# Macaron block on one core: Gram products of the projection stage in bursts of eight chunks instead of four, and the turns at a tile's end in another order

## The chip, the cores and the metric

The kernel is one program on one core of a Trainium2 chip. The metric is device time in microseconds (us) of one execution, and lower is better. Five engines run their own instruction streams and meet at semaphores: TensorE (PE in the profile, PEld for its weight loads), VectorE (DVE), ScalarE (ACT), GpSimd (POOL) and SyncE (SP), which here only issues DMAs.

## What is computed

The input is `x` of 1 x 8192 x 512 in fp32. A block of three parts works on it:

```
x = x + 0.5 * ffn(layernorm(x))
x = x + attn_block(layernorm(x))
x = x + 0.5 * ffn(layernorm(x))

ffn(x):   s = x @ Win + bin                       # 512 -> 64
          h = relu(s[..., None] * W1 + b1)        # 16 per hidden unit
          g = sum(h * W2) + b2;  g @ Wout + bout  # 64 -> 512
attn_block(x): gated delta rule with 16 heads of 32:
          q, k, v = rmsnorm(x) @ wq, wk, wv;  k = k / |k|;  beta = sigmoid(... @ wbeta)
          per token:  S += beta * (v - S k) k^T;   o = S q
          x + o @ wo, and then a 512 -> 2048 -> 512 MLP with its own rmsnorm and residual
```

The delta rule is computed in chunks of 32 tokens. For each chunk and head the kernel needs two 32 x 32 products beforehand: `K (beta K)^T`, masked to one strict triangle with the sign turned, and `Q (beta K)^T`, masked to the other triangle with its diagonal. These are the Gram products of this case.

## The kernel before

The kernel has three stages, one after the other: projections (stage 1, to about 1190 us), the delta rule over chunks (stage 2), and the MLP with the second ffn (stage 3). The change touches stage 1 alone.

Stage 1 runs over 16 tiles of 512 tokens (`NT` = 16, `t` below). Every engine's order is written out by hand, and work of neighbouring tiles is interleaved. While TensorE projects tile `t`, it also does the first ffn of tile `t + 1` (`hidden`, `ffn_out`) and most Gram products of tile `t - 1`. The engines' parts for one tile are:

- TensorE: thirteen projections `project(t, 0)` to `project(t, 12)` of 12 matmuls each (beta, then v, q, k for each of the four head groups `g4`), in PSUM banks 0 to 2 in turn. `hidden(t + 1)` stands between projections 1 and 2. `ffn_out(t + 1)`, four blocks in banks 6, 7, 6, 7, follows project(t, 6). Gram bursts `gram(t - 1, n)` use banks 6 and 7 in turn: four before and after project(t, 4) (two each), the same around projections 7 and 10.
- At a tile's end a list, `TURNS`, sets the order of the transposes of the next tile's normalised rows (`turn_h`, "h"), of those of the tile after next (`turn_x`, "x"), and of the first four Gram bursts of tile `t` ("g"). All three engines walk through this list: TensorE does the transposes and Gram bursts, ScalarE `h_turned` and `x_turned`, VectorE `h_low` (for "h") and `mask` (for "g").
- VectorE: `mask(t, n)` multiplies the finished burst by the two triangles, two instructions of 128 columns (`ltb`, line 765, and `pb`, line 767). The bank is free for the next use once the second is done (`released[bk] = v_P, ...`). VectorE also does the ffn's sums over hidden units (`sums`, line 670), the transposes of v and k (`turn_v`, line 727, `turn_k`, line 734, `turn_kb`, line 756), bias and residual adds (`add_bout`, line 658, `add_ffn`, line 677) and key norms (`norms`, line 738).
- `h_low(t + 1, f)` (line 713) writes the low part of the next tile's projection operand and frees the bank of turn_h (banks 3, 4, 3, 5 for f = 0 to 3). Turns "x" use banks 5, 4, 3, 4. The next tile's projections need all four parts.
- SyncE: `store_gram(t)` writes `ltb` and `pb` out, 1 MB each, once the last mask of tile `t` is done; `store_v`, `store_q` of the next tile and `load_x` stand behind it in the same queue. `mask(t, 0)` overwrites the buffers and so waits for both stores of tile `t - 1`.

On TensorE a burst and its bank look so before the change:

```
bk, g4 = 6 + n % 2, n // 4
...
bank_free(bk)
for i in range(4):
    for h in range(4):
```

Of the kernel before, what the change touches and what calls it, by code (L numbers as in the profile page):

```python
# [12 lines left out]
P = 128  # L13
# [9 lines left out]
CH = 32  # L23
# [15 lines left out]
def shape_constants():  # L39
# [17 lines left out]

H_BANK, X_BANK, WIN_BANK = (3, 4, 3, 5), (5, 4, 3, 4), 5

TURNS = (("h", 0), ("h", 1), ("x", 0), ("g", 0), ("h", 2), ("g", 1), ("x", 1), ("h", 3),  # L60
         ("g", 2), ("x", 2), ("g", 3), ("x", 3))


def solver_slots(systems):
# [23 lines left out]
def macaron(nc, a, consts, out, x1_d, z_d, heads_d, lt_d, xt_d):  # L88
# [28 lines left out]
    with ExitStack() as top:  # L117
# [115 lines left out]
        def sp_project(e):  # L233

            def load_x(t):
                i = t % 2
                if t >= 2:
                    e.wait_ge(d_x1[i], 16 * (t // 2))
                    e.wait_ge(a_y1, 4 * (t - 1))
                e.dma_start(X[i][:, :, :], x_v[t]).then_inc(d_x[i], 16)  # L240

            def store_x1(t):
                e.wait_ge(v_x1, 4 * t + 4)
                e.dma_start(x1_v[t], X[t % 2][:, :, :]).then_inc(d_x1[t % 2], 16)
# [12 lines left out]
            def store_q(t):  # L257
                e.wait_ge(a_ev, 13 * t + PROJ_AT["q", 3] + 1)
                e.dma_start(slot(t, Q2), chunked(qk[:, 0, :, :, :])).then_inc(d_q, 16)

            def store_k(t):
                e.wait_ge(v_kn, 4 * t + 4)
                e.dma_start(slot(t, K2), chunked(kb2[t % 2][:, :, :, :])).then_inc(d_k, 16)

            def store_b(t):
                e.wait_ge(o_kb, 4 * t + 4)
                e.dma_start(slot(t, B2), chunked(kbuf[:, :, :, :])).then_inc(d_b, 16)

            def store_gram(t):
                e.wait_ge(v_lt, 16 * t + 16)  # L270
                e.dma_start(lt_d[t // 2, :, (t % 2) * TC:(t % 2 + 1) * TC, :, :], ltb[:, :, :, :]).then_inc(d_lts, 16)
                e.wait_ge(v_P, 16 * t + 16)
                e.dma_start(slot(t, P2), chunked(pb[:, :, :, :])).then_inc(d_p, 16)

            def load_weights(i):
                j = i % 8
                if i >= 8:
                    e.wait_ge(v_wlo, i - 8 + 1)
                e.dma_start(stage1[j], pieces1[i][0]).then_inc(d_stage[j], 16)

            def load_system0(t):
                n = group_in(t)
                if n is not None:
                    e.wait_ge(d_lts, 32)
                    e.wait_ge(p_win, min(t + 2, NT))
                    e.dma_start(lt0, lt_d[0, :, :, n, :]).then_inc(d_lt0, 16)

            def store_system0(t):
                n = group_out(t)
                if n is not None:  # L290
                    e.wait_ge(v_back0, n + 1)
                    e.dma_start(xt_d[:, :, n, :].rearrange("c p i -> p c i"), xt0).then_inc(d_xt0, 16)

            load_x(0)
            load_x(1)
            e.wait_ge(o_z, 2)
            e.dma_start(wbraw[:, :, :], a["L0_attn_wbeta"].rearrange("(k p) h -> p k h", p=P)).then_inc(d_w1, 16)
            for h in range(4):
                e.dma_start(bbeta[32 * h:32 * h + GROUPS, :],
                            a["L0_attn_bbeta"].rearrange("(g h o) -> h g o", h=4, o=1)[h], **SHORT).then_inc(d_w1, 16)  # L300
            for n in KINDS:
                e.dma_start(bias[n][:, :], a[f"L0_attn_b{n}"].rearrange("(g p) -> p g", p=P),
                            **SHORT).then_inc(d_w1, 16)
            e.dma_start(ln1[:, :], a["L0_attn_ln1_scale"].rearrange("(g p) -> p g", p=P), **SHORT).then_inc(d_w1, 16)
            for i in range(8):
                load_weights(i)
            store_x1(0)
            for i in range(8, 12):
                load_weights(i)
            for t in range(NT):  # L310
                if t + 2 < NT:
                    load_x(t + 2)
                load_system0(t)
                if t:
                    store_k(t - 1)
                    store_b(t - 1)
                if t + 1 < NT:
                    store_x1(t + 1)
                store_system0(t)
                if t:  # L320
                    store_gram(t - 1)
                store_v(t)
                store_q(t)
            store_k(NT - 1)
            store_b(NT - 1)
            store_gram(NT - 1)

        def pe_project(e):
# [58 lines left out]

            def gram(t, n):

                bk, g4 = 6 + n % 2, n // 4  # L390
                e.wait_ge(v_kbT, 4 * t + g4 + 1)
                e.wait_ge(v_KT, 4 * t + g4 + 1)
                e.wait_ge(a_ev, 13 * t + PROJ_AT["q", g4] + 1)
                bank_free(bk)
                for i in range(4):
                    for h in range(4):
                        r, c = slice(32 * h, 32 * h + 32), 4 * (n % 4) + i
                        m = e.matmul(bank[bk][r, i * WIDE:(i + 1) * WIDE].rearrange("p (s i) -> p s i", s=2),  # L398
                                     rawk[r, c, g4, :], qk[r, :, c, g4, :], start=True, stop=True)
                m.then_inc(p_gram, 1)  # L400
                released[bk] = v_P, 16 * t + n + 1

            e.wait_ge(d_par, PAR)
            e.wait_ge(a_half, 2)
# [8 lines left out]
            for t in range(NT):  # L413
# [5 lines left out]
                project(t, 3)  # L419
                for g4 in range(1, GROUPS):  # L420
                    if t:
                        gram(t - 1, 4 * g4)
                        gram(t - 1, 4 * g4 + 1)
                    project(t, 3 * g4 + 1)
                    if t:
                        gram(t - 1, 4 * g4 + 2)
                        gram(t - 1, 4 * g4 + 3)
                    project(t, 3 * g4 + 2)
                    project(t, 3 * g4 + 3)
                    if g4 == 1 and t + 1 < NT:  # L430
# [1 line left out]
                for what, n in TURNS:  # L432
# [3 lines left out]
                        turn_h(t + 1, n)  # L436
                    elif what == "x" and t + 2 < NT:
                        turn_x(t + 2, n)
            for n in range(4, 16):
                gram(NT - 1, n)  # L440

        def act_project(e):
# [49 lines left out]
            def evict(t, j):  # L492
# [14 lines left out]
                elif kind == "q":  # L507
                    if t:
                        e.wait_ge(d_q, 16 * t)
                        e.wait_ge(p_gram, 16 * (t - 1) + 4 * g4 + 4)  # L510
                    e.activation(qk[:, 0, :, g4, :], blocks(bank[bk][:, :]), ACT.Identity,
                                 bias=bias[kind][:, g4:g4 + 1]).then_inc(a_ev, 1)
                else:
                    if t:
                        e.wait_ge(p_gram, 16 * (t - 1) + 4 * g4 + 4)
                    elif g4 == 0:
                        e.wait_ge(v_wb, 1)
                    e.activation(rawk[:, :, g4, :], blocks(bank[bk][:, :]), ACT.Identity,
# [115 lines left out]
        def dve_project(e):  # L634
# [105 lines left out]
            def scale_k(t, g4):  # L740
# [7 lines left out]
                e.tensor_tensor(K, K, nrm[:, u].unsqueeze(2).broadcast_to([P, TC, HD]), ALU.mult).then_inc(v_kn, 1)  # L748
                e.wait_ge(v_kn, n + 1)
                if t:  # L750
                    e.wait_ge(p_gram, 16 * (t - 1) + 4 * g4 + 4)
                e.transpose(qk[:, 1, :, g4, :], K).then_inc(v_KT, 1)

            def turn_kb(t, g4):
# [1 line left out]
                e.transpose(rawk[:, :, g4, :], kbuf[:, :, g4, :]).then_inc(v_kbT, 1)  # L756

            def mask(t, n):
                g4, c = n // 4, slice(4 * (n % 4), 4 * (n % 4) + 4)
                gb = bank[6 + n % 2][:, 0:4 * WIDE].rearrange("p (u s i) -> p u s i", s=2, i=CH)  # L760
                e.wait_ge(p_gram, 16 * t + n + 1)
                if t:
                    e.wait_ge(d_lts, 16 * t)
                    e.wait_ge(d_p, 16 * t)
                e.tensor_tensor(ltb[:, c, g4, :], gb[:, :, 1, :], gmask[:, 0:1, :].broadcast_to([P, 4, CH]),
                                ALU.mult).then_inc(v_lt, 1)
                e.tensor_tensor(pb[:, c, g4, :], gb[:, :, 0, :], gmask[:, 1:2, :].broadcast_to([P, 4, CH]),  # L767
                                ALU.mult).then_inc(v_P, 1)

            def system0(t):  # L770
# [68 lines left out]
            for t in range(NT):  # L839
# [26 lines left out]
                system0(t)  # L866
                turn_k(t, 0)
                if t:
                    mask(t - 1, 4)
                    mask(t - 1, 5)  # L870
                turn_v(t, 1)
                if t + 2 < NT:
                    add_bout(t + 2, 1)
                if t + 1 < NT:
                    sums(t + 1, 6, 7)
                if t:
                    mask(t - 1, 6)
                    mask(t - 1, 7)
                    turn_kb(t - 1, 3)
                if t + 2 < NT:  # L880
                    add_bout(t + 2, 2)
# [4 lines left out]
                    add_ffn(t + 1)  # L886
                turn_k(t, 1)
                if t:
                    mask(t - 1, 8)
                    mask(t - 1, 9)  # L890
                turn_v(t, 2)
                scale_k(t, 0)
                if t + 1 < NT:
                    stats_x1(t + 1, 0)
                    stats_x1(t + 1, 1)
                if t:
                    mask(t - 1, 10)
                    mask(t - 1, 11)
                if t + 1 < NT:
                    stats_x1(t + 1, 2)  # L900
                    stats_x1(t + 1, 3)
# [4 lines left out]
                    shift1(t + 1)  # L906
                turn_k(t, 2)
                if t:
                    mask(t - 1, 12)
                    mask(t - 1, 13)  # L910
                turn_v(t, 3)
                if t + 1 < NT:
                    scale_h(t + 1, 0)
                    scale_h(t + 1, 1)
                scale_k(t, 1)
                if t:
                    mask(t - 1, 14)
                    mask(t - 1, 15)
                if t + 1 < NT:
                    scale_h(t + 1, 2)  # L920
                    scale_h(t + 1, 3)
# [9 lines left out]
            norms(NT - 1, 3)  # L931
            turn_kb(NT - 1, 2)
            scale_k(NT - 1, 3)
            for n in range(4, 12):
                mask(NT - 1, n)
            turn_kb(NT - 1, 3)
            for n in range(12, 16):
                mask(NT - 1, n)

        def pool_project(e):  # L940
# [1061 lines left out]
```

## Time and profile before

| | |
|---|---|
| runs | 3695.51 us median of 3 (3686.24 to 3698.28) |
| the profiled execution | 3692.6 us, span 3690.6 us |
| TensorE busy | 3364.3 us, 91% of the span |
| VectorE, ScalarE, GpSimd busy | 1886.2, 1327.8, 1147.5 us |
| mean granted TensorE clock | 0.962 of full speed |
| stage 1 | its TensorE work ends near 1182 us, stage 2 begins its products at 1194 us |

The profile is of one execution. Busy times overlap between engines and are no parts of a sum. An engine's row in a timeline gives its start, its duration, and in brackets how long the engine was idle before it and who ended that. One fp32 matmul appears as two records; 64 records of line 398 are two Gram bursts of before.

### The profile page before, as it was taken

How to read it: one execution, taken by the hardware profiler on the slowest of the kernel's cores; microseconds unless marked ns; L12 is line 12 of the kernel's file. 1: busy time of each engine (PE TensorE's matmuls, PEld its weight loads, DVE VectorE, ACT ScalarE, POOL GpSimd, SP SyncE). 2: the span in 40 equal slices, each digit the busy share in tenths (PEclk: the TensorE clock that was granted, in tenths of full speed). 3: DMA queues.
4: the chain of work that ended last, by engine and by line, in shares of the span. 5: the costliest groups of instructions: out<-in, count | busy, mean ns of one | idle time of the engine just before them, and what ended most of it. 6: DMA issues, size and time to landing. Idle time of an engine off the chain costs nothing. (4 is left out here: it accounts for less than half of the span.)

```text
span 3690.6 us, 150931 instructions
## 1 busy us (share of the span) xinstructions
PE 3364.3 (91%) x68430; PEld 2637.4 (71%) x68430; DVE 1886.2 (51%) x3292; ACT 1327.8 (36%) x2630; POOL 1147.5 (31%) x1207
## 2 busy tenths in 40 slices
PE   3988888888896899999997899999999999999997
PEld 2666666666665688888886677777777777777775
DVE  4767766667664887877832233332333333333323
ACT  4434333344331233333333333333333333333332
POOL 0334435354452655555520112221121122122211
PEclk7999999999998899999998999999999999999998
DMA  3244353444334666665655110001000111000000
GB/s 90 81 150 121 105 159 115 115 137 133 110 122 143 196 193 192 200 192 182 187 173 167 65 35 24 23 35 35 24 35 35 35 35 35 35 30 17 35 35 23
DMA packets 388102, 355.46 MB, mean 96 GB/s; under 512 B 58128, under 2 KB 320912, under 8 KB 384912
## 3 DMA queue, kind: packets, MB, share of 16 engines
q1 hardware_dynamic: 385632, 351.27, 30.4%
q8 instruction: 155, 2.54, 0.3%
q10 hardware_dynamic: 2224, 0.90, 0.1%
q14 instruction: 91, 0.75, 0.1%
HBM read 184.19 MB, written 153.09 MB: 91 GB/s over the span
## 5 line engine op out<-in xcount | busy, mean ns | idle before, releaser
L1784 DVE TENSOR_TENSOR glo<-gl,gh 128x512 fp32r<-128x512 f32 x256 | 195.1, 762 | 927.3 <-ACT gh L1691 927.2
L1687 ACT ACTIVATE gl<-bank,b1m 128x512 f32<-128x512 f32 x256 | 175.9, 687 | 796.4 <-PE bank L231 796.4
L229 PE MATMUL bank<-w_hi,gh 128*128 128x512 f32 x1024 | 410.6, 401 | 24.3 <-DVE glo L1784 24.3
L229 PE MATMUL bank<-h_hi,w_hi 128*128 128x512 f32 x1024 | 425.9, 416 | 4.0 <-DVE w_lo L1828 4.0
L231 PE MATMUL bank<-w_hi,glo 128*128 128x512 f32 x1024 | 406.7, 397 | 0.0
L230 PE MATMUL bank<-h_lo,w_hi 128*128 128x512 f32 x1024 | 406.4, 397 | 0.0
L231 PE MATMUL bank<-h_hi,w_lo 128*128 128x512 f32 x1024 | 406.3, 397 | 0.0
L230 PE MATMUL bank<-w_lo,gh 128*128 128x512 f32 x1024 | 405.5, 396 | 0.0
L398 PE MATMUL bank<-qk,rawk 32*32 32x64 f32 x8192 | 166.4, 230 | 117.9 <-DVE pb L767 110.6
L398 PEld LDWEIGHTS bank<-qk,rawk 32*32 32x32 f32 x8192 | 138.4, 114 | 172.2 <-issue 170.6
L970 POOL TENSOR_TENSOR nrm<-nrm,cst 128x16 f32<-128x16 f32 x64 | 185.6, 2900 | 198.1 <-DVE nrm L738 197.8
L229 PEld LDWEIGHTS bank<-w_hi,gh 128*128 128x128 f32 x1024 | 192.8, 188 | 75.4 <-DVE glo L1784 31.3
L1189 PE MATMUL bank<-ringA 32*32 32x32 f32 x16512 | 237.8, 196 | 7.0 <-issue 4.1
L229 PEld LDWEIGHTS bank<-h_hi,w_hi 128*128 128x128 f32 x1024 | 193.3, 189 | 59.0 <-issue 10.8
L230 PEld LDWEIGHTS bank<-h_lo,w_hi 128*128 128x128 f32 x1024 | 193.4, 189 | 55.0 <-issue 10.8
L231 PEld LDWEIGHTS bank<-w_hi,glo 128*128 128x128 f32 x1024 | 193.3, 189 | 47.0
L231 PEld LDWEIGHTS bank<-h_hi,w_lo 128*128 128x128 f32 x1024 | 193.2, 189 | 46.2
L230 PEld LDWEIGHTS bank<-w_lo,gh 128*128 128x128 f32 x1024 | 193.6, 189 | 44.8
L1189 PEld LDWEIGHTS bank<-ringA 32*32 32x32 f32 x16512 | 198.4, 105 | 10.9 <-issue 4.4
L1878 POOL TENSOR_TENSOR ss<-ss,cst 128x4 f32<-128x4 f32 x16 | 16.3, 1017 | 576.4 <-DVE ss L1767 576.4
L1466 POOL TENSOR_TENSOR zb<-zb,bo 128x512 f32<-128x512 f32 x64 | 91.0, 1422 | 334.0 <-ACT zb L1332 334.0
L1391 DVE TENSOR_TENSOR tmp<-sysf 128x90 f32<-128x90 f32 (+14 forms) x210 | 184.5, 879 | 5.0
(172 smaller groups left out, 7214.8 us busy)
## 6 DMA issues: line engine op xcount, KB each, us to landing
ringB<-heads_scratch SPq DMA_DIRECT2D x256, 192.0 KB, 2.7
ringA<-heads_scratch SPq DMA_DIRECT2D x258, 128.0 KB, 2.2
X<-in_L_attn_x SPq DMA_DIRECT2D x16, 1024.0 KB, 9.7
x_scratch<-X SPq DMA_DIRECT2D x16, 1024.0 KB, 5.5
heads_scratch<-vb SPq DMA_DIRECT2D x16, 1024.0 KB, 11.3
heads_scratch<-qk SPq DMA_DIRECT2D x16, 1024.0 KB, 11.0
heads_scratch<-kb SPq DMA_DIRECT2D x16, 1024.0 KB, 5.2
heads_scratch<-kbuf SPq DMA_DIRECT2D x16, 1024.0 KB, 7.7
```

The lines of the kernel that those rows point to most:

```text
L229: e.matmul(o, lhs[0], rhs[0], start=first, stop=False)
L230: e.matmul(o, lhs[0], rhs[1], start=False, stop=False)
L231: return e.matmul(o, lhs[1], rhs[0], start=False, stop=last)
L398: m = e.matmul(bank[bk][r, i * WIDE:(i + 1) * WIDE].rearrange("p (s i) -> p s i", s=2), rawk[r, c, g4, :], qk[r, :, c, g4, :], start=True, ...
L970: e.tensor_tensor(nrm[:, u], nrm[:, u], pos_half.broadcast_to([P, TC]), ALU.pow).then_inc(o_pow, 1)
L1189: m = e.matmul(out[r, n, :], lhsT[r, n, :], rhs[r, n, :], start=first and n == 0, stop=True, skip_group_check=True)
L1391: e.tensor_tensor(tt, N[:, :, j + 1:CH, j:j + 1].broadcast_to([P, 3, rows, j]), N[:, :, j:j + 1, 0:j].broadcast_to([P, 3, rows, j]), ALU.m ...
L1466: e.tensor_tensor(zb[i][:, :], zb[i][:, :], bo[:, :], ALU.add).then_inc(o_yb, 1)
L1687: e.activation(gl[k][:, :], bank[k][:, :], ACT.Gelu_apprx_tanh, bias=b1m[:, m:m + 1]).then_inc(a_gl, 1)
L1784: e.tensor_tensor(gh[k][1][:, :], gl[k][:, :], gh[k][0][:, :], ALU.subtract).then_inc(v_gl, 1)
L1878: e.tensor_tensor(ss3[:, :], ss3[:, :], neg_half, ALU.pow).then_inc(o_ms, 1)
```

## The change

A burst now takes eight chunks and fills its bank (512 columns), so a tile has `NG` = 8 bursts instead of 16, two for each head group. Even `n` goes to bank 6 and odd `n` to bank 7, so the two halves of a group stand in different banks. The mask instructions are 256 columns wide, and there are half as many. Only the first chunk of a burst carries the start flag. In `TURNS` there are two bursts instead of four, and the second stands behind all four "h". The stores and the waits on `p_gram` count in eights.

```diff
-TURNS = (("h", 0), ("h", 1), ("x", 0), ("g", 0), ("h", 2), ("g", 1), ("x", 1), ("h", 3),
-         ("g", 2), ("x", 2), ("g", 3), ("x", 3))
+TURNS = (("h", 0), ("h", 1), ("x", 0), ("g", 0), ("h", 2), ("x", 1), ("h", 3), ("g", 1), ("x", 2), ("x", 3))
+
+NG = 2 * GROUPS
...
-                bk, g4 = 6 + n % 2, n // 4
+                bk, g4 = 6 + n % 2, n // 2
...
-                for i in range(4):
+                for i in range(8):
                     for h in range(4):
-                        r, c = slice(32 * h, 32 * h + 32), 4 * (n % 4) + i
+                        r, c = slice(32 * h, 32 * h + 32), 8 * (n % 2) + i
...
-                                     rawk[r, c, g4, :], qk[r, :, c, g4, :], start=True, stop=True)
+                                     rawk[r, c, g4, :], qk[r, :, c, g4, :], start=i == 0, stop=True,
+                                     skip_group_check=True)
                 m.then_inc(p_gram, 1)
-                released[bk] = v_P, 16 * t + n + 1
+                released[bk] = v_P, NG * t + n + 1
...
                     if t:
-                        gram(t - 1, 4 * g4)
-                        gram(t - 1, 4 * g4 + 1)
+                        gram(t - 1, 2 * g4)
                     project(t, 3 * g4 + 1)
                     if t:
-                        gram(t - 1, 4 * g4 + 2)
-                        gram(t - 1, 4 * g4 + 3)
+                        gram(t - 1, 2 * g4 + 1)
...
-                e.tensor_tensor(ltb[:, c, g4, :], gb[:, :, 1, :], gmask[:, 0:1, :].broadcast_to([P, 4, CH]),
+                e.tensor_tensor(ltb[:, c, g4, :], gb[:, :, 1, :], gmask[:, 0:1, :].broadcast_to([P, 8, CH]),
...
-            for n in range(4, 12):
+            for n in range(2, 6):
                 mask(NT - 1, n)
             turn_kb(NT - 1, 3)
-            for n in range(12, 16):
+            for n in range(6, NG):
                 mask(NT - 1, n)
```

TensorE in the middle of tile 1, around project(1, 4) (the matmuls on `wv_hi`; rows of its other matmuls left out), before. Each burst is 16 matmuls, the waits stand in brackets, and `v_P` is the mask that frees the bank:

```order
L398 MATMUL bank6<-qk,rawk 32x64 [waits a_ev,v_P,v_KT,v_kbT]
L398 MATMUL bank6<-qk,rawk 32x64 x15
L398 MATMUL bank7<-qk,rawk 32x64 [waits a_ev,v_P,v_KT,v_kbT]
L398 MATMUL bank7<-qk,rawk 32x64 x15
L229 MATMUL bank2<-hT_hi,wv_hi 128x512 [waits a_ev,v_lo]
...
L398 MATMUL bank6<-qk,rawk 32x64 [waits a_ev,v_P,v_KT,v_kbT]
L398 MATMUL bank6<-qk,rawk 32x64 x15
L398 MATMUL bank7<-qk,rawk 32x64 [waits a_ev,v_P,v_KT,v_kbT]
L398 MATMUL bank7<-qk,rawk 32x64 x15
L229 MATMUL bank0<-hT_hi,wq_hi 128x512 [waits a_ev,v_lo]
```

The same place of the change:

```order
L399 MATMUL bank6<-qk,rawk 32x64 [waits a_ev,v_P,v_KT,v_kbT]
L399 MATMUL bank6<-qk,rawk 32x64 x31
L230 MATMUL bank2<-hT_hi,wv_hi 128x512 [waits a_ev,v_lo]
...
L399 MATMUL bank7<-qk,rawk 32x64 [waits a_ev,v_P,v_KT,v_kbT]
L399 MATMUL bank7<-qk,rawk 32x64 x31
L230 MATMUL bank0<-hT_hi,wq_hi 128x512 [waits a_ev,v_lo]
```

The matmuls ahead of and behind project(1, 4) are as many as before, but the burst behind it goes to bank 7, which was last used at the end of the tile before and not by the burst ahead of it.

TensorE at the end of tile 0, from the first Gram burst of the list on to the next tile's first matmul, before (`cst,Y1` is a turn "h", `cst,Y0` a turn "x"):

```order
L398 MATMUL bank7<-qk,rawk 32x64 x15
L341 MATMUL bank4<-cst,Y0 128x128 [waits v_lo,a_y0]
L341 MATMUL bank4<-cst,Y0 128x128 x3
L350 MATMUL bank5<-cst,Y1 128x128 [waits a_xT,v_h]
L350 MATMUL bank5<-cst,Y1 128x128 x3
L398 MATMUL bank6<-qk,rawk 32x64 [waits a_ev,v_P,v_KT,v_kbT]
L398 MATMUL bank6<-qk,rawk 32x64 x15
L341 MATMUL bank3<-cst,Y0 128x128 [waits v_lo,a_y0]
L341 MATMUL bank3<-cst,Y0 128x128 x3
L398 MATMUL bank7<-qk,rawk 32x64 [waits a_ev,v_P,v_KT,v_kbT]
...
L229 MATMUL bank1<-hT_hi,wb_hi 128x512 [waits a_ev,v_lo]
```

And in the change:

```order
L342 MATMUL bank4<-cst,Y0 128x128 [waits v_lo,a_y0]
L342 MATMUL bank4<-cst,Y0 128x128 x3
L351 MATMUL bank5<-cst,Y1 128x128 [waits a_xT,v_h]
L351 MATMUL bank5<-cst,Y1 128x128 x3
L399 MATMUL bank7<-qk,rawk 32x64 [waits a_ev,v_x1,v_KT,v_kbT]
L399 MATMUL bank7<-qk,rawk 32x64 x31
L342 MATMUL bank3<-cst,Y0 128x128 [waits v_lo,a_y0]
L342 MATMUL bank3<-cst,Y0 128x128 x3
L342 MATMUL bank4<-cst,Y0 128x128 [waits a_xT,a_y0]
L342 MATMUL bank4<-cst,Y0 128x128 x3
L230 MATMUL bank1<-hT_hi,wb_hi 128x512 [waits a_ev,v_lo]
```

The last burst moved ahead of the last two "x", and no burst of the list waits any more for a mask of the same list; the third "x" still waits for the third `h_low` (`v_lo`).

VectorE at the same tile's end, from the first two `h_low` on, before:

```order
L713 SCALAR_TENSOR_TENSOR hT_lo<-bank,ln,hT_hi 128x512 [waits a_hi] x2
L765 TENSOR_TENSOR ltb<-bank,cst 128x4x32 [waits p_gram]
L767 TENSOR_TENSOR pb<-bank,cst 128x4x32
L713 SCALAR_TENSOR_TENSOR hT_lo<-bank,ln,hT_hi 128x512 [waits a_hi]
L765 TENSOR_TENSOR ltb<-bank,cst 128x4x32 [waits p_gram]
L767 TENSOR_TENSOR pb<-bank,cst 128x4x32
L713 SCALAR_TENSOR_TENSOR hT_lo<-bank,ln,hT_hi 128x512 [waits a_hi]
```

And in the change:

```order
L713 SCALAR_TENSOR_TENSOR hT_lo<-bank,ln,hT_hi 128x512 [waits a_hi] x2
L765 TENSOR_TENSOR ltb<-bank,cst 128x8x32 [waits p_gram]
L767 TENSOR_TENSOR pb<-bank,cst 128x8x32
L713 SCALAR_TENSOR_TENSOR hT_lo<-bank,ln,hT_hi 128x512 [waits a_hi] x2
L765 TENSOR_TENSOR ltb<-bank,cst 128x8x32 [waits p_gram]
L767 TENSOR_TENSOR pb<-bank,cst 128x8x32
```

One mask, now twice as wide, still stands between the second and the third `h_low`, as before; the one between the third and the fourth is gone.

## Rows read from the trace of the kernel before

**Rows 1.** The page, busy time: us, share, instructions

```profile
PE 3364.3 (91%) x68430; PEld 2637.4 (71%) x68430; DVE 1886.2 (51%) x3292; ACT 1327.8 (36%) x2630; POOL 1147.5 (31%) x1207
```

**Rows 2.** Waits of stage 1, 80 to 1180 us: total, times, longest

```profile
PE bank L398 <- DVE pb L767: 110.6, 32, 6.8
...
DVE ltb L765 <- DMA heads_scratch<-pb: 55.6, 15, 4.7
...
PE bank L367 <- DVE X L677: 15.2, 14, 1.1
...
PE bank L398 <- DVE X L677: 2.9, 14, 0.2
```

**Rows 3.** Timeline of TensorE, middle of tile 7: start, duration, idle before

```profile
561.62 0.40 PE L231 MATMUL bank<-hT_hi,wv_lo 128*128 128x512 f32 x1
566.05 1.93 PE L398 MATMUL bank<-qk,rawk 32*32 32x64 f32 x64 [4.04 <-DVE pb L767]
...
575.02 1.88 PE L367 MATMUL bank<-wout,g 128*128 128x512 f32 x4
577.99 1.98 PE L367 MATMUL bank<-wout,g 128*128 128x512 f32 x4 [1.09 <-DVE X L677]
```

**Rows 4.** Timeline of VectorE, the same stretch of tile 7

```profile
565.46 0.25 DVE L765 TENSOR_TENSOR ltb<-bank,cst 128x128 f32<-128x128 f32 x1
...
566.23 0.68 DVE L727 STREAM_TRANSPOSE vb<-proj 128x512 f32<-128x512 f32 x1
566.84 0.64 DVE L658 TENSOR_TENSOR X<-X,boutb 128x512 f32<-128x512 f32 x1
567.41 1.59 DVE L670 SCALAR_TENSOR_TENSOR g<-relu,w2t,g 128x512 f32<-128x512 f32 x2
568.92 0.28 DVE L765 TENSOR_TENSOR ltb<-bank,cst 128x128 f32<-128x128 f32 x1
...
569.72 0.70 DVE L756 STREAM_TRANSPOSE rawk<-kbuf 128x512 f32<-128x512 f32 x1
573.85 0.69 DVE L658 TENSOR_TENSOR X<-X,boutb 128x512 f32<-128x512 f32 x1 [3.43 <-ACT Y L449]
```

**Rows 5.** Windows from the waiting burst to ffn_out's third block, tiles 1 to 13: length, busy, clock

```profile
221.07:230.78 9.71, 8.62 (x92) 1.00 0.30 88
...
711.44:724.01 12.57, 11.48 (x92) 0.75 0.00 1
...
sum 150.69, PE 136.54; mean PE 10.50
```

**Rows 6.** Timeline of TensorE, middle of tile 14, the last with an ffn_out

```profile
1061.38 1.10 PE L398 MATMUL bank<-qk,rawk 32*32 32x64 f32 x64 [1.76 <-DVE pb L767]
```

**Rows 7.** Timeline of TensorE, end of tile 7

```profile
610.42 0.65 PE L398 MATMUL bank<-qk,rawk 32*32 32x64 f32 x32 [3.45 <-DVE pb L767]
...
613.13 0.78 PE L229 MATMUL bank<-hT_hi,wb_hi 128*128 128x512 f32 x1
```

**Rows 8.** Timeline of SyncE's queue, end of tile 7: the store of P

```profile
600.86 0.44 SPq L273 DMA_DIRECT2D heads_scratch<-pb  x1
```

**Rows 9.** Timeline of VectorE, end of tile 7

```profile
609.78 0.29 DVE L765 TENSOR_TENSOR ltb<-bank,cst 128x128 f32<-128x128 f32 x1 [4.53 <-DMA heads_scratch<-pb]
...
610.19 0.74 DVE L713 SCALAR_TENSOR_TENSOR hT_lo<-bank,ln,hT_hi 128x512 fp32r<-128x512 f32 x1
```

**Rows 10.** Windows of 7 us behind a tile-end wait (two) and behind ffn_out's wait (one): clock is the fourth number

```profile
540.86:547.86 7.00, 6.99 (x93) 1.00 0.98 280
...
1035.73:1042.73 7.00, 7.00 (x81) 0.55 0.81 238
...
577.99:584.99 7.00, 6.77 (x120) 1.00 0.40 152
```

**Rows 11.** Timeline of VectorE, end of stage 1

```profile
1157.62 0.29 DVE L765 TENSOR_TENSOR ltb<-bank,cst 128x128 f32<-128x128 f32 x1 [4.20 <-DMA heads_scratch<-pb]
...
1168.00 0.25 DVE L765 TENSOR_TENSOR ltb<-bank,cst 128x128 f32<-128x128 f32 x1
...
1182.02 0.28 DVE L767 TENSOR_TENSOR pb<-bank,cst 128x128 f32<-128x128 f32 x1
```

More of the change, by code:

```diff
@@ L269, in store_gram @@
             def store_gram(t):
-                e.wait_ge(v_lt, 16 * t + 16)
+                e.wait_ge(v_lt, NG * t + NG)
                 e.dma_start(lt_d[t // 2, :, (t % 2) * TC:(t % 2 + 1) * TC, :, :], ltb[:, :, :, :]).then_inc(d_lts, 16)
-                e.wait_ge(v_P, 16 * t + 16)
+                e.wait_ge(v_P, NG * t + NG)
                 e.dma_start(slot(t, P2), chunked(pb[:, :, :, :])).then_inc(d_p, 16)
@@ L438, in pe_project @@
                         turn_x(t + 2, n)
-            for n in range(4, 16):
+            for n in range(2, NG):
                 gram(NT - 1, n)
@@ L509, in evict @@
                         e.wait_ge(d_q, 16 * t)
-                        e.wait_ge(p_gram, 16 * (t - 1) + 4 * g4 + 4)
+                        e.wait_ge(p_gram, NG * (t - 1) + 2 * g4 + 2)
                     e.activation(qk[:, 0, :, g4, :], blocks(bank[bk][:, :]), ACT.Identity,
@@ L514, in evict @@
                     if t:
-                        e.wait_ge(p_gram, 16 * (t - 1) + 4 * g4 + 4)
+                        e.wait_ge(p_gram, NG * (t - 1) + 2 * g4 + 2)
                     elif g4 == 0:
@@ L750, in scale_k @@
                 if t:
-                    e.wait_ge(p_gram, 16 * (t - 1) + 4 * g4 + 4)
+                    e.wait_ge(p_gram, NG * (t - 1) + 2 * g4 + 2)
                 e.transpose(qk[:, 1, :, g4, :], K).then_inc(v_KT, 1)
@@ L758, in mask @@
             def mask(t, n):
-                g4, c = n // 4, slice(4 * (n % 4), 4 * (n % 4) + 4)
-                gb = bank[6 + n % 2][:, 0:4 * WIDE].rearrange("p (u s i) -> p u s i", s=2, i=CH)
-                e.wait_ge(p_gram, 16 * t + n + 1)
+                g4, c = n // 2, slice(8 * (n % 2), 8 * (n % 2) + 8)
+                gb = bank[6 + n % 2][:, :].rearrange("p (u s i) -> p u s i", s=2, i=CH)
+                e.wait_ge(p_gram, NG * t + n + 1)
                 if t:
@@ L764, in mask @@
                     e.wait_ge(d_p, 16 * t)
-                e.tensor_tensor(ltb[:, c, g4, :], gb[:, :, 1, :], gmask[:, 0:1, :].broadcast_to([P, 4, CH]),
+                e.tensor_tensor(ltb[:, c, g4, :], gb[:, :, 1, :], gmask[:, 0:1, :].broadcast_to([P, 8, CH]),
                                 ALU.mult).then_inc(v_lt, 1)
-                e.tensor_tensor(pb[:, c, g4, :], gb[:, :, 0, :], gmask[:, 1:2, :].broadcast_to([P, 4, CH]),
+                e.tensor_tensor(pb[:, c, g4, :], gb[:, :, 0, :], gmask[:, 1:2, :].broadcast_to([P, 8, CH]),
                                 ALU.mult).then_inc(v_P, 1)
@@ L868, in dve_project @@
                 if t:
-                    mask(t - 1, 4)
-                    mask(t - 1, 5)
+                    mask(t - 1, 2)
                 turn_v(t, 1)
@@ L876, in dve_project @@
                 if t:
-                    mask(t - 1, 6)
-                    mask(t - 1, 7)
+                    mask(t - 1, 3)
                     turn_kb(t - 1, 3)
@@ L888, in dve_project @@
                 if t:
-                    mask(t - 1, 8)
-                    mask(t - 1, 9)
+                    mask(t - 1, 4)
                 turn_v(t, 2)
@@ L896, in dve_project @@
                 if t:
-                    mask(t - 1, 10)
-                    mask(t - 1, 11)
+                    mask(t - 1, 5)
                 if t + 1 < NT:
@@ L908, in dve_project @@
                 if t:
-                    mask(t - 1, 12)
-                    mask(t - 1, 13)
+                    mask(t - 1, 6)
                 turn_v(t, 3)
@@ L916, in dve_project @@
                 if t:
-                    mask(t - 1, 14)
-                    mask(t - 1, 15)
+                    mask(t - 1, 7)
                 if t + 1 < NT:
```

## The prediction

> **What bounds the kernel now.** I read the page first: TensorE is busy for 91% of the span [rows 1], so only its idle time, its slow stretches and the path that feeds it are worth anything. Stages 2 and 3 are untouched by the change. For stage 1 the next view is the list of waits. There, one wait stands out for TensorE: 110.6 us in 32 times until a mask's second instruction frees a Gram bank [rows 2]. The timeline shows that this comes twice a tile, at different places and for different reasons.
>
> The first place is the middle of the tile, in tiles 1 to 14. The bursts behind project(t, 4) need the banks of the bursts ahead of it. VectorE comes to those masks only behind its sums for the ffn. In tile 7 TensorE's last matmul before starts at 561.62 us and the burst at 566.05, with 4.04 us idle [rows 3]. The wait is 2.9 us in tiles 1 and 2, 1.76 in tile 14 [rows 6], and up to 6.7 where VectorE also has a system of the solver to transpose. After it the granted clock is mostly low: from the waiting burst to the third block of `ffn_out` tile 2 takes 9.71 us at clock 1.00, tile 9 takes 12.57 us at 0.75, and thirteen tiles together take 150.69 us [rows 5].
>
> The second place is the tile's end. VectorE waits there for the store of P of the tile before (15 times, 55.6 us [rows 2]), in tile 7 until 609.78 us, 4.53 us long [rows 9]. That store is issued at 600.86, behind the last mask [rows 8]. TensorE waits behind it for 3.45 us and starts the next tile at 613.13 [rows 7].
>
> **The middle of the tile.** The matmuls stay: a burst of eight chunks has those of two bursts. What goes is the wait, since the burst behind project(t, 4) is now in bank 7, whose last mask was done at the end of the tile before. TensorE then runs ahead, and the next thing that it needs of VectorE is in `ffn_out`: block 0 needs the last of the sums and bank 6, block 1 bank 7, block 2 the first `add_ffn`. I work this out in tile 7, with G = 566.05 as the mark.
>
> - TensorE alone: the burst would start at G - 4.04, last about 1.0, then two projections of 12 matmuls at 0.235 us, 5.6 in all. It reaches `ffn_out` at G + 2.6 instead of G + 8.97 (575.02). Block 2 followed 2.97 us behind block 0 [rows 3], so G + 5.6 were possible.
> - VectorE: the four masks at 565.46 take 0.77 us to 566.23. Two of double width: no row shows one of 256 columns, so I bound it. Starts of 128-column masks are 0.19 to 0.20 apart, 512-column adds 0.57 to 0.61 [rows 4]; between the two lies 0.33 for 256 columns, 0.67 for the pair (bounds: 0.4, no more than one of before each, and 0.8, no saving). So turn_v starts 0.1 earlier. Then turn_v 0.61, an add of bout 0.57, sums 1.51, which end at G + 2.8; masks 0.67, turn_kb 0.63, and four instructions of 0.6 (add, norms, add, the first `add_ffn`). That ends at about G + 6.55, and block 2 starts at G + 6.65. ScalarE's rows that these adds wait for, 3.43 us in the trace [rows 4], hang on projections 5 and 6, which are done earlier; this wait goes.
>
> So VectorE sets the new time: G + 6.65 against G + 11.94 in tile 7, 5.3 us less. For thirteen tiles the sum is 150.69 - 13 x 6.65 = 64.2 us. In tile 14 no adds of bout are in the way; its 1.76 us and about 1.3 of slow clock go, 3 us. The 0.21 us that the second burst behind `ffn_out` waits for the last add, 14 times, 2.9 us [rows 2], go too, as that burst now stands behind project(t, 7).
>
> Behind this, two shorter idle times are left: about 0.35 us before block 0 (3 us in tiles 6, 9 and 12, with the solver's transposes) and 1.8 before block 2, where 1.09 stand now. What do they cost in clock? Behind the 1.09 us idle the granted clock was 1.00 in all thirteen tiles [rows 10]. Behind the ten idle times of 2.0 to 2.6 us at tile ends it was 1.00 in five, as after tile 6, and 0.55 to 0.78 in five [rows 10]. With 1.8 us, between the two, I take a slow stretch in 5 of 14 tiles. One costs 1.6 us, about the difference of a usual tile's 11.3 to the 9.71 of tile 2 [rows 5]: 8 us lost.
>
> The trace thus puts a price on each idle time by the clock behind it. The Trainium skill (TensorE: Matmul & The Clock Gate, "A second HAM failure mode: psum-queue depth-cycling") says that an engine which goes through PSUM banks with small idle times between its groups may fall back and forth between the two clocks. By that rule every `ffn_out` would be followed by a slow stretch; the rows behind 1.09 us idle do not agree. It is the first rival below.
>
> **The tile's end.** VectorE still meets its first mask of the list, and the wait for the store, ahead of the third `h_low`; this wait is not removed. With D = 609.78: the mask now takes 0.67, the third `h_low` 0.66 to 0.74, so the third "x" can start at D + 1.5, the fourth at D + 2.0, the next tile at D + 2.6. Now it is 613.13, D + 3.35. That is 0.7 us less, since the second burst's 8 chunks are done before the wait instead of two bursts of 4 within or behind it. TensorE's idle time stays, about 0.3 us longer, and slow stretches behind it fall wholly on projections. I take 0.5 us in 14 tiles, 7 us (bounds 0 and 12). The store is issued where it was, one mask pair's 0.1 us earlier.
>
> **The last tile.** From 1157.62 to 1168.00 us VectorE has four mask pairs and two chains of key scaling; the first two bursts are done before, so that 1.7 us of alternating go. From 1168.00 to 1182.02 there are eight mask pairs, each in turn with a burst [rows 11]. With wider bursts half the hand-overs remain; worked out with 1.93 us for eight chunks at the slow clock [rows 3] it is 10.4 us instead of 14. But TensorE has an idle time there of 2.8 us in which it waits for nothing that the profile shows, and it may stay. So 2.8 to 5.5 us in all; I take 4.
>
> **The sum.** 64.2 + 3.0 + 2.9 - 8 + 7 + 4 = 73.1 us. Against the profiled execution's 3692.6 us this gives 3619.5. The median of the runs is 2.9 us above it, so I forecast 3621 us for the median, 2.0% less. Half as many mask instructions save VectorE some 0.1 us a pair elsewhere; that lies behind TensorE and is counted at nothing. If a mask were as dear as its upper bound, each tile would lose 0.25 us, 3 us in all.
>
> **Rivals.**
> 1. The shorter idle times bring the clock down in every tile. For it speak the five slow cases at 2.0 to 2.6 us, and that the idle time before block 0 comes on top; against it the 1.00 behind 1.09 us. Then 14 x 1.6 = 22 us are lost instead of 8: 3635 us, up to 3645 if the tile's end gives nothing.
> 2. No change: what the middle gains is waited for at the tile's end, if the stores' landing kept a time of its own. For it: VectorE's 15 waits on the store [rows 2]. Against it: the store is issued behind the tile's last mask [rows 8], which moves along with TensorE, and it takes the same 8.9 us to D. It gives 3690.
> 3. Slower: a store of P takes longer to land. It shares the queue with stores of V and Q and the load of x, and the DMA engines were 0.98 busy in such a stretch [rows 10]. A tile shorter by 5 us brings these nearer to those of the last tile. If the 8.9 us grew by more than 5.2, the gain of the middle would be used up; at 8 us more the kernel takes 14 x 2.8 = 39 us longer, 3731 us. Against it: between two tile ends the DMAs are busy for well under half the time (shares 0.18 to 0.40 in the middle windows), so there is room.
> 4. The wide bursts change nothing of the middle's wait, because bank 7 would not be free. Its last mask stands at the end of the tile before and 25 us earlier, so I give this almost nothing; it would leave 11 us of gain, 3684.
>
> **How the numbers follow.** The forecast 0.70, rival 1 0.18, rival 2 0.04, rival 3 0.05, rival 4 0.03. A measurement of this kernel tells about 0.3% (11 us) from no change. Faster by more is the forecast, rival 1 and part of rival 4, 0.90; within it 0.05; slower 0.05. The range goes on the fast side to no loss of clock and the tile end's 12 us (3608, and 6 less for the runs' spread, 3602); on the slow side over rival 1 with nothing at the tile's end to 3650.
>
> **What would show it.** In the profile after, the mid-tile burst should have no idle time before it, VectorE should have no 3.4 us wait for ScalarE before its adds, and block 2 of `ffn_out` should wait 1.5 to 2 us for `add_ffn`, with a clock near 1.00 behind it in most tiles. At the tile's end TensorE should wait 3 to 4 us for `h_low` before the third "x". Stage 1 should end near 1110 us. I am wrong if VectorE is so late with the sums that block 0 waits 3 us in all tiles, if the mask of 256 columns takes well over 0.4 us, or if the wait for the store of P grows.

## The result and the profile after

The changed kernel takes 3611.5 us (median of 4 runs, 3609.9 to 3613.7), the kernel before beside it 3696.9 us. The ratio is 0.9768, with a 95% interval of 0.9753 to 0.9782: 2.3% less. The forecast was 3621 us, 2.0% less, and a range of 3602 to 3650.

The page of the kernel after, against [rows 1]: TensorE is busy for 29 us less with the same number of instructions, and VectorE has 256 instructions fewer.

```profile
span 3608.1 us, 150299 instructions
...
PE 3335.6 (92%) x68430; PEld 2614.6 (72%) x68430; DVE 1865.4 (52%) x3036; ACT 1325.0 (37%) x2630; POOL 1151.6 (32%) x1207
```

TensorE's waits from 80 to 1110 us in the kernel after (total, times, longest), to be read against [rows 2]:

```profile
PE bank L342 <- DVE hT_lo L713: 27.3, 13, 2.8
PE bank L368 <- DVE X L677: 17.2, 12, 1.7
PE bank L368 <- DVE g L670: 11.6, 8, 3.1
PE bank L399 <- issue: 11.0, 5, 2.3
PE bank L399 <- DVE pb L767: 9.7, 2, 5.4
```

The bursts' wait for a mask is down from 110.6 us in 32 times to 9.7 in 2, both in the work of the last tile. Instead, the tile's end has TensorE wait 13 times for the third `h_low` (27.3 us), and in the middle `ffn_out` waits for `add_ffn` (17.2) and for the sums (11.6). Four of the five idle times in the row "issue" are new too: at the end of tiles 1, 5, 9 and 13 TensorE stops for 2.0 to 2.3 us inside a burst, for nothing that the profile shows. These stops lie ahead of the third `h_low`, which TensorE has to wait for anyway; what makes them stays open.

The timeline of TensorE around `ffn_out` and at the end of tile 7 shows both waits, against [rows 3] and [rows 7]:

```profile
533.62 1.10 PE L399 MATMUL bank<-qk,rawk 32*32 32x64 f32 x64
...
540.62 1.99 PE L368 MATMUL bank<-wout,g 128*128 128x512 f32 x4
544.27 1.99 PE L368 MATMUL bank<-wout,g 128*128 128x512 f32 x4 [1.67 <-DVE X L677]
...
572.26 1.09 PE L399 MATMUL bank<-qk,rawk 32*32 32x64 f32 x64
575.54 1.07 PE L342 MATMUL bank<-cst,Y 128*128 128x128 f32 x8 [2.19 <-DVE hT_lo L713]
```

The burst behind project(t, 4) has no idle time before it. VectorE's timeline at the same places, against [rows 4] and [rows 9]:

```profile
537.15 0.38 DVE L765 TENSOR_TENSOR ltb<-bank,cst 128x256 f32<-128x256 f32 x1
...
540.48 0.41 DVE L765 TENSOR_TENSOR ltb<-bank,cst 128x256 f32<-128x256 f32 x1
540.82 0.41 DVE L767 TENSOR_TENSOR pb<-bank,cst 128x256 f32<-128x256 f32 x1
541.15 0.70 DVE L756 STREAM_TRANSPOSE rawk<-kbuf 128x512 f32<-128x512 f32 x1
541.77 0.65 DVE L658 TENSOR_TENSOR X<-X,boutb 128x512 f32<-128x512 f32 x1
...
573.99 0.42 DVE L765 TENSOR_TENSOR ltb<-bank,cst 128x256 f32<-128x256 f32 x1 [2.87 <-DMA heads_scratch<-pb]
```

The adds of bout follow without the 3.43 us of waiting for ScalarE. Within a pair the two mask instructions start 0.34 us apart, and the pair takes 0.67 us.

Where did the time go? I cut tiles 1 to 13 into three windows each: from the tile's first projection matmul to `ffn_out`'s first block, from there to the first turn at the tile's end, and from there to the next tile. These are the sums over thirteen tiles, with TensorE's busy time beside them; first, second and third window in this order. Before:

```profile
sum 420.97, PE 361.78; mean PE 27.83
...
sum 353.23, PE 336.09; mean PE 25.85
...
sum 133.85, PE 94.45; mean PE 7.27
```

After:

```profile
sum 355.56, PE 343.72; mean PE 26.44
...
sum 357.08, PE 340.49; mean PE 26.19
...
sum 120.01, PE 83.52; mean PE 6.42
```

So the first part is 65.4 us shorter, of which 47.4 are idle time (59.2 down to 11.8) and 18.1 busy time of the same matmuls, which now run at a higher clock. The second is 3.9 us longer, the third 13.8 shorter, so that the three together are 75.4 us shorter. Tiles 0, 14, 15 and the end of stage 1 give 15.2 us more: stage 2's first products start at 1103.5 instead of 1194.1. From there on the two programs are the same. Their rows, before and after (length, then busy time of TensorE, its weight loads, VectorE, ScalarE and GpSimd, then the granted clock):

```profile
1194.10:3690.60 2496.50, 2380.34 (x56972) 1906.56 (x56972) 1113.57 (x1504) 886.06 (x1957) 686.59 (x731) 0.98 0.26 84
```

```profile
1103.50:3608.10 2504.60, 2383.67 (x56972) 1909.98 (x56972) 1113.11 (x1504) 886.11 (x1957) 685.77 (x731) 0.98 0.26 84
```

That part took 8.1 us more in the profile after. In the profiles of the nine experiments it took 2499.6 to 2506.1 us, and 2505.7 in that of e1, whose stage 1 is nearly as long as before. So I read it as a spread of stages 2 and 3 and not as something that the change does, though there is only one profile of the kernel before. That profile, at 3692.6 us, was itself below the medians of 3696.9 to 3699.7 us that the kernel before had beside the change and the experiments.

### The profile page after: what moved, and what is told of

The parts are those of the page before. It is cut to its first block and busy times, and to the rows that moved or that the text cites. A ratio compares the mean times of both kernels' runs of the same rounds, so it can differ in the third digit from the quotient of the medians.

```text
span 3608.1 us, 150299 instructions
## 1 busy us (share of the span) xinstructions
PE 3335.6 (92%) x68430; PEld 2614.6 (72%) x68430; DVE 1865.4 (52%) x3036; ACT 1325.0 (37%) x2630; POOL 1151.6 (32%) x1207
## 5 line engine op out<-in xcount | busy, mean ns | idle before, releaser
L1389 DVE TENSOR_TENSOR sysf<-sysf,tmp 128x90 f32<-128x90 f32 (+14 forms) x210 | 183.5, 874 | 6.4
L1881 POOL TENSOR_TENSOR Z<-Z,H 128x512 f32<-128x512 f32 x64 | 91.9, 1436 | 283.2 <-DMA H<-x_scratch 283.2
```

The source lines that it names most:

```text
L1389: e.tensor_tensor(N[:, :, j + 1:CH, 0:j], N[:, :, j + 1:CH, 0:j], tt, ALU.add).then_inc(v_sol, 1)
L1881: e.tensor_tensor(z[:, b, :], z[:, b, :], H[:, b, :], ALU.add).then_inc(o_zx, 1)
```

## The experiments

Theory: the gain is the middle's, since the burst behind project(t, 4) finds its bank free; VectorE's chain then sets `ffn_out`. Rival: fewer and wider instructions and fewer hand-overs give it. Medians of the kernel before lay between 3698.8 and 3699.7 us beside these runs. "The change" below is the changed kernel at 3611.5 us, and e1 to e9 are edits of it.

### e1: the bank alone undone

```diff
-                bk, g4 = 6 + n % 2, n // 2
+                bk, g4 = 6 + (n % 2 if n != 3 else 0), n // 2
```

The mask reads the same bank.

> The changed kernel, with the burst behind project(t, 4) and its mask in bank 6 instead of bank 7, so that it again waits for the mask of the burst ahead of project(t, 4). Widths, counts and the list of turns stay as changed. Theory (the gain of the tile's middle comes from the bank being free): the wait of 3 to 4 us before that burst and the slow clock behind it are back, 4 to 5 us in each of 14 tiles, so 3611 + 55 to 70 = 3666 to 3681 us. Rival (the gain comes from fewer and wider mask instructions and fewer hand-overs): no more than 15 us back, under 3626.

Measured: 3688.1 us, ratio 0.9968 (0.9957 to 0.9980) to before. The bank alone is worth 76.6 of the 87.6 us that lie between the kernel before, 3699.0 us beside this run, and the change. Its windows, in the same order:

```profile
sum 432.58, PE 369.02; mean PE 28.39
...
sum 347.68, PE 333.28; mean PE 25.64
...
sum 119.45, PE 83.44; mean PE 6.42
```

The first part is back and even 11.6 us longer than before; the third stays short. Of the 11.6 us, 5.1 stand between the tile's first matmul and VectorE's first mask of the middle, and 6.5 between that mask and `ffn_out`; what makes them was not tried by itself. The rival falls: with all widths, counts, start flags and the list as changed, only 11 us are left, about what the tile's end gives. The upper end of the theory, 3681 us, was 7 us too low.

### e2: masks of 128 columns

```diff
+                for i in range(2):
...
-                e.tensor_tensor(ltb[:, c, g4, :], gb[:, :, 1, :], gmask[:, 0:1, :].broadcast_to([P, 8, CH]),
+                    m = e.tensor_tensor(ltb[:, w, g4, :], gb[:, u, 1, :], gmask[:, 0:1, :].broadcast_to([P, 4, CH]),
```

> The changed kernel with each mask made of four instructions of 128 columns instead of two of 256; banks and order as changed. In the profile after, starts of 256-column masks are 0.33 us apart, those of 128 columns 0.19 to 0.20 before, so a pair costs 0.11 us more for VectorE. Two pairs lie on the path to ffn_out's blocks, one ahead of the store, one ahead of the third h_low. Theory (width is a small term): 0.3 to 0.4 us in 14 tiles, 4 to 6 us more, 3615 to 3617. Rival (width carries the gain): over 20 us more.

Measured: 3626.0 us, 14.5 more than the change, between theory and rival. Its windows:

```profile
sum 360.50, PE 348.01; mean PE 26.77
...
sum 358.46, PE 340.67; mean PE 26.21
...
sum 128.37, PE 84.45; mean PE 6.50
```

The first two parts are 4.9 and 1.4 us longer, as the width predicts. The other 8.4 us are at the tile's end, 7.4 of them idle time of TensorE (36.5 up to 43.9). VectorE has only 0.1 us more to do there ahead of the third `h_low` and 0.1 ahead of the store, 3 us in thirteen tiles. The trace shows where some of the rest is: from the issue of the store of P to the mask that waits for it, tiles 2 and 10 took 9.50 and 9.47 us in e2, and 8.04 and 8.01 in the change. So in these two the store landed later. Why it did these runs don't settle, and with it not whether those 3 us come of the narrow masks.

### e3: the second burst behind the last turn

```diff
-TURNS = (("h", 0), ("h", 1), ("x", 0), ("g", 0), ("h", 2), ("x", 1), ("h", 3), ("g", 1), ("x", 2), ("x", 3))
+TURNS = (("h", 0), ("h", 1), ("x", 0), ("g", 0), ("h", 2), ("x", 1), ("h", 3), ("x", 2), ("x", 3), ("g", 1))
```

> The changed kernel with the second burst of the list behind the fourth x turn instead of ahead of the third, on TensorE; VectorE's order is as changed. Theory (TensorE waits there for the store of P, and what stands ahead of the wait is free): 1.1 us of burst moves from the idle time to behind it, 1.1 us at the full clock and up to 1.9 at the slow one, so 13 tiles lose 15 to 25 us, 3626 to 3636. Rival (the next tile's first projection is bound by VectorE's h_low and not by TensorE, so that the order is neutral): within 5 us of 3611.

Measured: 3633.8 us, 22 more than the change, within the theory's range. The timeline of TensorE in e3, end of tile 7, shows the burst behind a wait of 3.18 us, where the kernel after waits 2.19 us with the burst already done:

```profile
588.35 1.06 PE L342 MATMUL bank<-cst,Y 128*128 128x128 f32 x8 [3.18 <-DVE hT_lo L713]
589.34 1.09 PE L399 MATMUL bank<-qk,rawk 32*32 32x64 f32 x64
590.37 0.51 PE L230 MATMUL bank<-hT_hi,wb_hi 128*128 128x512 f32 x1
```

### e4: both masks behind all h_low

On VectorE only:

```diff
-                for what, n in TURNS:
-                    if what == "g":
-                        mask(t, n)
-                    elif what == "h" and t + 1 < NT:
-                        h_low(t + 1, n)
+                for n in range(NF if t + 1 < NT else 0):
+                    h_low(t + 1, n)
+                mask(t, 0)
+                mask(t, 1)
```

> The changed kernel with both masks of a tile's end behind all four h_low on VectorE; TensorE and ScalarE as changed. This takes the wait for the store of P out of the way of the next tile's operand. Theory A (that wait alone holds TensorE at the tile's end, some 2.2 us idle and in half the tiles a slow clock behind it): the next tile starts 2.2 to 3 us earlier in 13 tiles, 35 to 45 us less, 3566 to 3576. Rival B (the load of x stands behind the stores in the same queue, landed 1.5 us late at one tile already, and does not move along): VectorE waits for it instead at the row statistics, 2 us or more longer, ffn_out comes as late as before, and most is given back: 3590 to 3608.

Measured: 3591.7 us, ratio 0.9705 (0.9689 to 0.9722) to before, 19.8 us less than the change. That is within rival B's range, and the windows bear it out: the tile's end is 29 us shorter (90.65 against 120.01), but the first part is 14 us longer (369.88 against 355.56), and the list of waits of e4 (80 to 1090 us) says why:

```profile
DVE stats L638 <- DMA X<-in_L_attn_x: 30.9, 10, 4.4
...
PE bank L368 <- DVE g L670: 28.4, 10, 6.2
```

VectorE waits for the load of x, and `ffn_out` for the sums, 28.4 us instead of 11.6.

### e5: and the load of x ahead of the stores of V and Q

This is e4 with an edit of SyncE's queue:

```diff
+            load_x(2)
             for t in range(NT):
-                if t + 2 < NT:
-                    load_x(t + 2)
...
                 if t:
                     store_gram(t - 1)
+                if t + 3 < NT:
+                    load_x(t + 3)
                 store_v(t)
                 store_q(t)
```

> The kernel of the run before (both masks behind all h_low), and in SyncE's queue the load of x for the tile after next stands ahead of the stores of V and Q instead of behind them. Theory (the load of x took back the gain: 30.9 us of waits on it and 28 us of waits of ffn_out's first block for the sums): these waits go, ffn_out comes 1 us or more earlier in 13 tiles and slow stretches with it, 12 to 25 us less, 3567 to 3580. Rival (the ring as a whole is late, so that V's or Q's store is waited for by turn_v or by the eviction of q instead): within 5 us of 3592.

Measured: 3584.7 us, 7.0 less than e4: between theory and rival. VectorE's wait for the load of x (30.9 us in e4) is gone from the list of waits, but `ffn_out` still waits for the sums, and VectorE for the store of V:

```profile
PE bank L369 <- DVE g L671: 18.6, 9, 4.2
...
DVE vb L728 <- DMA heads_scratch<-vb: 11.6, 6, 2.6
```

The store of V, now behind the load, is late for `turn_v`. The DMA engines are busy for 0.90 to 0.97 of the third windows of e5. I take from this that the queue is near its limit at a tile's end, and that the place in it mostly chooses who waits; no run took a transfer out to show it.

### e6: the adds ahead of turn_kb and norms

```diff
-                    turn_kb(t - 1, 3)
                 if t + 2 < NT:
                     add_bout(t + 2, 2)
-                norms(t, 0)
-                if t + 2 < NT:
                     add_bout(t + 2, 3)
                 if t + 1 < NT:
                     add_ffn(t + 1)
+                if t:
+                    turn_kb(t - 1, 3)
+                norms(t, 0)
```

> The changed kernel with turn_kb(t - 1, 3) and norms(t, 0) on VectorE behind add_ffn instead of ahead of it. Theory (VectorE's chain behind the sums sets ffn_out's third block, which waits 1.67 us): block 2 comes 0.65 us after block 0 earlier, until TensorE's own 2.97 us, the least seen, is reached: 13 x 0.65 = 8 us less, 3601 to 3605. Rival (ScalarE's normalised rows, which the adds of bout wait for, hold it anyway): no gain, 3608 to 3615.

Measured: 3599.3 us, 12.2 less than the change. The theory said 8, so the gain is 4 us larger. The part behind `ffn_out`'s first block shrinks by 11.0 us:

```profile
sum 346.08, PE 338.70; mean PE 26.05
```

### e7: the solver's transposes behind add_ffn

```diff
                     sums(t + 1, 4, 5)
-                system0(t)
...
                     add_ffn(t + 1)
+                system0(t)
                 turn_k(t, 1)
```

> The changed kernel with the transposes of the solver's systems behind add_ffn on VectorE. Theory (in tiles 3, 6, 9 and 12 they make ffn_out's first block wait 0.9 to 3.1 us and bring a slow clock of 0.56 to 0.78 behind it): 3 tiles gain 3 us and 1.5 of slow clock each, one gains 0.9, 12 to 16 us less, 3595 to 3600. Rival (the sums end late in these tiles for another reason, or GpSimd's solve now starts too late and is waited for): under 4 us.

Measured: 3597.5 us, 14.0 less than the change, within the theory's range. The first part is 13.0 us shorter and has almost no idle time left:

```profile
sum 342.60, PE 341.52; mean PE 26.27
```

The second is 4.1 us shorter as well, and the third 4.5 longer. Tile 6 has 2.5 us of that; there the store of P landed 9.27 us behind its issue, and 8.02 us in the change.

### e8: the four edits together

> The four edits together: masks behind all h_low, load of x ahead of V and Q, the adds ahead of turn_kb and norms, systems behind these. If each wait is a place of its own, the gains add: 20 for the masks, 12 to 25 for the load, 8 for the adds, 12 to 16 for the systems: 3542 to 3560. Rival (VectorE's chain from the tile's start to the sums sets ffn_out once TensorE is early, and takes part of it back): 3565 to 3575.

The edits of e4, e5, e6 and e7, with the systems behind `turn_kb` and `norms`. Measured: 3563.1 us, ratio 0.9634 (0.9617 to 0.9651) to before, and the fastest of all. It is 48 us less than the change, where the edits one by one give 26.8 (e4 and e5 together), 12.2 and 14.0, in all 53. So they almost add up, 3 us above the theory's range and 2 below the rival's.

### e9: the last group's key scaling behind the adds too

Against e8. The last hunk is GpSimd's order, where `root(t, 0)` moves ahead of a step of the solver:

```diff
-                if t:
-                    scale_k(t - 1, 3)
...
                     add_ffn(t + 1)
                 if t:
-                    turn_kb(t - 1, 3)
+                    scale_k(t - 1, 3)
...
                     mask(t - 1, 4)
+                    turn_kb(t - 1, 3)
...
-                system0(t, 1)
                 root(t, 0)
+                system0(t, 1)
```

> The four edits together, and on VectorE the scaling of the last group's keys, scale_k(t - 1, 3), behind add_ffn instead of ahead of the sums, turn_kb(t - 1, 3) behind the next mask, and on GpSimd root(t, 0) ahead of the solver's steps. Theory (with an early tile start, VectorE's chain of statistics, key scaling and sums sets ffn_out's first block, 1 to 2 us late in most tiles): 1.9 us of work leave this chain, the first block comes 1 to 1.7 us earlier in 8 to 10 tiles and at the full clock, 10 to 20 us less than the 3563 of the four edits: 3543 to 3553. Rival (the chain is held by ScalarE's relus or by what TensorE itself takes, and the scaling only fills a wait): within 5 us of 3563.

Measured: 3575.8 us, 13 more than e8: a miss. The first part is 5.8 us shorter than in e8 (344.48 against 350.25), so the chain was shortened, but the second is 13.8 us longer (361.86 against 348.10). The list of waits of e9 shows where:

```profile
POOL kbuf L973 <- DMA heads_scratch<-kbuf: 38.8, 13, 6.4
...
DVE Y L709 <- POOL ri L952: 19.3, 15, 1.7
...
PE bank L352 <- DVE Y L709: 17.9, 13, 2.7
```

GpSimd's product for the keys now waits for the buffer's store. Its row statistics stand behind that in its order, so VectorE's scaled rows for the turns come late: the lower two rows are 5.8 us in 4 times and 4.0 in 4 times in e8. The chain is read from the waits; `root` and the keys were not moved one without the other.

## Why the prediction was right

- **The mechanism of the middle** was right in each step. The wait went, VectorE became what sets `ffn_out`'s third block, the wait for ScalarE vanished, and block 2 waits 1.67 us (1.8 said). e1 shows that the bank is the cause, e6 and e7 that VectorE's order sets the rest. The size was right too. From VectorE's first mask in the middle of the tile to block 2, tile 7 took 12.53 us before (577.99 less 565.46) and takes 7.12 now (544.27 less 537.15), which in the prediction's marks is G + 6.53 where it had G + 6.65. In tiles 1 to 13 this stretch is 65.4 us shorter, where the sum had 64.2.
- **The loss of clock** is the term that was mis-sized: 8 us in the sum. Behind the idle time of 1.67 us, the granted clock was 1.00 in all eight tiles that show it, as in the two with 1.1 us. It fell only in tiles 6, 9 and 12, where the first block waits 3.1 us for the sums: to 0.78, 0.56 and 0.76 in the 7 us behind. Even there block 2 started 3.65 us behind block 0, as in the other tiles, since it waits for VectorE anyway; only tile 9 has a longer second part, by 1.8 us. So rival 1 is out. The rule that the prediction cites from the Trainium skill (TensorE: Matmul & The Clock Gate, "A second HAM failure mode: psum-queue depth-cycling") says that going through PSUM banks with small idle times may send the clock back and forth; these ten do not bear it out, since going through banks 6 and 7 with such idle times cost no clock. The length of the idle time does not decide alone either. The prediction took 1.8 us to lie between its rows at 1.09 and at 2.0 us, and passed over its own nearest row: the 1.76 us in tile 14 of the kernel before, behind which the clock was 0.76. In e3, two of the three idle times of 3.1 us were followed by 1.00. The windows behind three of the ten:

```profile
289.07:296.07 7.00, 6.98 (x144) 1.00 0.40 149
...
544.27:551.27 7.00, 6.99 (x144) 1.00 0.40 150
...
929.63:936.63 7.00, 6.98 (x144) 1.00 0.39 149
```

Behind the 3.1 us in tiles 6 and 9:

```profile
478.50:485.50 7.00, 6.86 (x73) 0.78 0.01 2
668.58:675.58 7.00, 6.38 (x8) 0.56 0.00 0
```

Behind the 1.76 us in tile 14 of the kernel before:

```profile
1061.38:1068.38 7.00, 7.00 (x83) 0.76 0.63 186
```

And behind 3.1 us in tiles 9 and 12 of e3:

```profile
683.70:690.70 7.00, 5.32 (x73) 1.00 0.00 0
...
882.04:889.04 7.00, 5.31 (x73) 1.00 0.00 0
```

- **The tile's end** gave what was said, 6.5 us in thirteen tiles, though the windows hide it. The third window is 13.8 us shorter, but it ends at the next tile's first matmul. Slow stretches behind the wait now fall wholly on the projections that follow, as the prediction had it, and so from the tile's first matmul to VectorE's first mask in the middle it takes 308.6 us instead of 301.1 in the thirteen tiles, 7.5 more. (In tile 4, where the clock behind the wait fell from 1.00 to 0.76, it is 1.2 us more, and in tile 8, where it rose from 0.76 to 1.00, 0.9 less.) Net it is 6.3 us. In tile 7 the next tile starts 2.38 us behind the first mask (575.54 + 0.83 against 573.99) where I had 2.6, and before it was 3.35. e3 gives the price of the second burst's place, 22 us, more than I had credited the move with.
- **A near match by chance.** With its loss of clock the sum has 59.5 us for the first two windows of thirteen tiles (64.2 + 2.7 - 7.4), and they give 65.4 - 3.9 = 61.5. But the 7.4 us of clock did not come; what stands in their place is the 7.5 us ahead of the first mask, which the sum had booked at the tile's end.
- **The last tiles** gave 15.2 us with the first, where I had 7.1. Tile 14 alone is 8.5 us shorter, where about 3 were said: its end has no "x", and with the burst ahead, only the next projection's third part waits for the store. That projection starts at 1020.59, and 1.71 us are waited for behind its first six matmuls. I had treated the tile like the others.
- **What I left out** is the spread of stages 2 and 3. The sum was made against one profile in which they took 2496.5 us, the least of all profiles, and the change's took 2504.6. The gain in stage 1 is 90.6 us, 17.5 more than the sum, and 82.5 in the two spans. So the time came nearer to the forecast than stage 1 did, which is luck. The last step of the sum is off as well: 3619.5 + 2.9 is 3622.4, and not 3621.
- **Rivals 2 to 4** did not come. For rival 2, the tile's end kept nothing of the middle's gain: VectorE's wait for the store is 53.1 us in 15 times against 55.6. For rival 3, from the store's issue to the mask that waits for it took 7.5 to 9.2 us in the kernel after and 7.5 to 9.1 before, 8.2 and 8.1 on average. (The shares of the DMA engines in the middle windows of before, given there as 0.18 to 0.40, are 0.00 to 0.30 in the trace.) For rival 4, the burst in bank 7 had no idle time before it. But e4 shows that rival 2 was near: once the tiles start two or three us earlier still, a transfer that does not come earlier takes part of the gain back.

The version that the experiments point to, e8, takes 3563 us, 1.3% less than the change and 3.7% less than the kernel before.

## What to carry to other kernels

When two buffers are used in turn and an engine waits for the one just used, count which instruction frees it and what stands ahead of that on its engine: a different assignment of buffers can take the wait away at no change in work (e1: 76.6 of 87.6 us). When a wait at a handover point can't be removed, put work that doesn't depend on it ahead (e3), and keep what others need from standing behind it (e4). And after each such step list what the shortened engine asks for next; here it was VectorE's order, then the DMA queue.

## What the runs showed of the hardware

TensorE's granted clock was 1.00 (its upper level, 2.4 GHz) in the 7 us behind each idle time of 1.1 and 1.7 us ahead of `ffn_out`'s third block, in ten of the tiles 1 to 13 of the changed kernel, and behind 1.09 us in all thirteen before. Behind the nine undivided idle times of 2.2 to 2.8 us at tile ends of the changed kernel it was 1.00 in five and 0.76 in four, and behind the three of 3.1 us it was 0.56 to 0.78, part of the time at the lower level (1.2 GHz). The length does not decide alone: in the kernel before, 1.76 us in tile 14 were followed by 0.76 and 2.90 us in tile 2 by 1.00, and in e3 two of three idle times of 3.1 us by 1.00.

A mask of 256 columns from PSUM costs VectorE 0.31 to 0.34 us from start to start, against 0.19 to 0.20 for one of 128 and about 0.6 for an add of 512.

The mask that waits for the store of P, 1 MB issued together with others at a tile's end, started 7.5 to 9.2 us behind that store's issue in both kernels, in most tiles close to 7.5, 8.0 or 9.1.

Stages 2 and 3, the same instructions in each kernel, took between 2496.5 and 2506.1 us from profile to profile, so one profile of each kernel can be 10 us off in a comparison of spans.
